# Causal mask of an attention's row maxima: two of four query blocks moved from products on TensorE to a fused add-and-minimum on VectorE

## The chip, the cores and the metric

The kernel runs on one core of a Trainium2 chip. The metric is device microseconds of one execution; less is better. The engines are TensorE (PE; PEld is its weight load), VectorE (DVE), ScalarE (ACT), GpSimd (POOL) and SyncE (SP, which issues most DMAs). A line number, as L626, is that of the kernel's file.

## What is computed

One transformer layer on `x` of (4, 512, 256) with a context of (4, 1601, 256): an attention of 16 heads of 16 columns each, causal, and behind it a layer norm and a feed-forward block with 8 experts (two for each row) and a shared one. The change lies in the attention:

```python
scores = jnp.einsum('bhqd,bhkd->bhqk', Q, K) / jnp.sqrt(jnp.float32(dk))
causal = jnp.tril(jnp.ones((Sq, Sk), dtype=bool))
scores = jnp.where(causal, scores, -jnp.inf)
attn = jax.nn.softmax(scores, axis=-1)
out = jnp.einsum('bhqk,bhkd->bhqd', attn, V)
```

Because of the mask only the first 512 rows of the context count.

## The kernel before

**Groups and slots.** A batch has 512 queries (four blocks k of 128) and 16 heads, handled in four groups of four heads: 16 groups in all, numbered 0 to 15 here in the order in which their maxima are found. For each group the kernel computes the scores twice. First with the queries on the partitions, only to find each row's maximum (kind "R", `rowmax_scores` at L616 on TensorE, `rowmax` at L1296 on VectorE). Then with the keys on the partitions (kind "S", `scoresT` at L638), where the negated maximum of each query is already in the operands as three more rows, so that ScalarE's exponential at L1074 can follow directly, GpSimd clears what lies above the diagonal (L528), and TensorE multiplies with the values (kind "PV", `probs_v`, L654).

**R jobs.** A group has six: two of query block 3 (two heads of 512 keys each), two of block 2 (two heads of 384), one of block 1 (four heads of 256), one of block 0 (four heads of 128); they are called R0 to R5 below, in this order. For each head TensorE makes a product of queries and keys (L624, 96 rows deep, since the float32 operands are split into bf16 parts) and adds to its last 128 columns a product of the identity with a mask tile (L626) that holds 0 up to the diagonal and -1e30 above it. VectorE then reduces the whole job in one instruction to the negated maximum of each row and head (L1306). The jobs alternate between two pairs of accumulator banks (`set_a`): TensorE's job n waits at L617 until VectorE has freed job n - 2.

**From the maxima to the operands.** When all six are reduced, `max_parts` splits the 16 columns of maxima into three bf16 parts (four small instructions, L1312 to L1318). TensorE transposes them (kind "MAX", `maxima`, L634), ScalarE copies the result (L995 called from L1035) and sends it by DMA (L1038) into the operand rows of that group's S jobs.

**The order on TensorE** is written out by hand. In a slot the S jobs of one group, the PV jobs of the group before and the R jobs of the group after are interleaved:

```python
SLOT = [("R", 0), ("PV", 0), ("R", 1), ("PV", 1), ("R", 2),
        ("S", 0), ("R", 3), ("S", 1), ("R", 4), ("S", 2), ("S", 3), ("R", 5), ("S", 4), ("S", 5),
        ("S", 6), ("S", 7), ("PV", 2), ("PV", 3), ("S", 8), ("MAX", 0), ("S", 9), ("S", 10)]
```

The eleven S jobs and the MAX job rotate through three banks (`set_b`); job n waits (L639) until job n - 3 has been read. Every second middle slot is followed by, or follows, the projections of the next batch's queries and keys (L675), and ScalarE splits these into parts within the slot (the copies of L1014 between its exponentials). A batch ends with transposes (L807) and the output projection (L832). The first group's R jobs have no slot around them. After the attention come routing and the experts, which the change doesn't touch.

**Constants.** GpSimd fills the identity, the mask and other constants at the start (L464 to L480); TensorE waits for them (L686) and then repeats a product without use (L684, `keep_busy`) until its first input is there.

Of the kernel before, what the change touches and what calls it, by code (L numbers as in the profile page):

```python
# [28 lines left out]
P = 128  # L29
F32 = mybir.dt.float32  # L30
F32R = mybir.dt.float32r
BF16 = mybir.dt.bfloat16
I32 = mybir.dt.int32
ALU = mybir.AluOpType
ACT = mybir.ActivationFunctionType
AX = mybir.AxisListType
# [3 lines left out]
MASKED = -1e30  # L40
LOWEST = -3e38
# [3 lines left out]
def build(nc, x, ctxT, wqT, bq, wkT, bk, wvT, bv, woT, bo, gwT, wupT, wdnT, sgT, suT, sdT, out):  # L45
    B, S, D = x.shape
    H = NUM_HEADS
    DK = D // H
    HG = P // 32
# [25 lines left out]
    ROWS = DK * len(Q_PART)  # L75
# [4 lines left out]
    with ExitStack() as ctx:  # L80
        def sb(name, shape, dt=F32):
            return ctx.enter_context(nc.sbuf_tensor(name, shape, dt))

        def sem(name):
            return ctx.enter_context(nc.semaphore(name))
# [8 lines left out]
        A = ctx.enter_context(nc.psum_tensor("set_a", [P, 4, 512], F32))  # L94
# [11 lines left out]
        gw = sb("gate_w", [P, C, 32])  # L106
        ident = sb("ident", [P, P])
        identb = sb("identb", [P, P], BF16)
        maskb = sb("maskb", [P, P], BF16)
        beforeb = sb("beforeb", [P, P], BF16)  # L110
        onesb = sb("onesb", [P, P], BF16)
        expert_of = sb("expert_of", [P, NT], I32)
# [40 lines left out]
        def part(words):  # L153
            lo = used[0]
            used[0] += words
            assert used[0] <= size[0], used[0] / KB
            return region[0][:, lo:lo + words]
# [10 lines left out]
        qstack = part(2 * HH * S // 2).bitcast(BF16).rearrange("p (a h n) -> p a h n", a=2, h=HH)  # L168
        kstack = part(2 * HH * S // 2).bitcast(BF16).rearrange("p (a h n) -> p a h n", a=2, h=HH)
# [5 lines left out]
        mneg = part(QT * HG).rearrange("p (k h) -> p k h", k=QT)  # L175
# [15 lines left out]
        bqc = part(2)  # L191
        bkc = part(2)
        zeros = part(D + WHO)

        xs = [attn, attnT.rearrange("p c (k d) -> p (c k) d", d=D)]

# [26 lines left out]
        tot, tiles_of, ends, base = (part(E) for _ in range(4))  # L223
# [24 lines left out]
        consts, pads, fills, pad_rows = sem("consts"), sem("pads"), sem("fills"), sem("pad_rows")  # L248
# [13 lines left out]

        a_full, a_free, b_full, b_free = sem("a_full"), sem("a_free"), sem("b_full"), sem("b_free")
        p_masked, rc_ready, pool_turns = sem("p_masked"), sem("rc_ready"), sem("pool_turns")

        lt_full, lt_read, lg_read, logits_full, route, d_ready, ex_ready, sel_ready = (sem(n) for n in
            ("lt_full", "lt_read", "lg_read", "logits_full", "route", "d_ready", "ex_ready", "sel_ready"))
# [49 lines left out]

        assert A_ALL % 2 == 0
        MAX_AT = 9
        FIRST = [("R", 0), ("R", 1), ("R", 2), ("S", 0), ("R", 3), ("S", 1), ("R", 4), ("S", 2), ("R", 5)]  # L320
        FIRST += [(kind, n) for kind, n in SLOT if kind == "MAX" or kind == "S" and n > 2]
        for order in (SLOT, FIRST):
# [19 lines left out]
        def pair(bank_set, n):  # L342
            return bank_set[:, n % 2 * 2:n % 2 * 2 + 2, :]
# [118 lines left out]
        def _(pool):  # L462
            g = nc.gpsimd
# [2 lines left out]
            g.affine_select(out=ident[:], in_=ident[:], compare_op=ALU.not_equal, fill=1.0, base=0,  # L466
                            pattern=[[-1, P]], channel_multiplier=1).then_inc(consts, 1)
            g.memset(identb[:], 0.0).then_inc(pads, 1)
            g.memset(maskb[:], 0.0).then_inc(pads, 1)
            g.memset(beforeb[:], 0.0).then_inc(pads, 1)  # L470
            g.memset(onesb[:], 1.0).then_inc(pads, 1)
            g.memset(gw[:], 0.0).then_inc(pads, 1)
# [1 line left out]
            g.affine_select(out=identb[:], in_=identb[:], compare_op=ALU.not_equal, fill=1.0, base=0,  # L474
                            pattern=[[-1, P]], channel_multiplier=1).then_inc(consts, 1)

            g.affine_select(out=maskb[:], in_=maskb[:], compare_op=ALU.is_ge, fill=MASKED, base=0,
                            pattern=[[-1, P]], channel_multiplier=1).then_inc(consts, 1)

            g.affine_select(out=beforeb[:], in_=beforeb[:], compare_op=ALU.is_ge, fill=1.0, base=0,  # L480
# [122 lines left out]
        def _(pe):  # L603
            mm, tr = nc.tensor.matmul, nc.tensor.transpose
# [11 lines left out]
            def rowmax_scores(g, j, n, par):  # L616
                pe.wait_ge(a_free, n - 1)  # L617
                k, h0, heads = R_JOBS[j]
                w = (k + 1) * P
                in_bank = heads // 2 if k else HG  # L620
                for i in range(heads):
                    h = g % 2 * HG + h0 + i
                    dst = pair(A, par)[:, i // in_bank, i % in_bank * w:(i % in_bank + 1) * w]
                    mm(dst, qstack[0:ROWS, g // 2, h, k * P:w], kstack[0:ROWS, g // 2, h, 0:w],  # L624
                       start=True, stop=False)
                    last = mm(dst[:, k * P:w], identb[:], maskb[:], start=False, stop=True)  # L626
                last.then_inc(a_full, 1)

            def maxima(n, par, g_count, first=False):
# [236 lines left out]
            last = [logits(b) for b in range(B - 1)][-1]  # L866
# [20 lines left out]
            for t in range(T):  # L887
                last = mm(Bk[:, 3, 0:E], onesb[:], selb[:, t, :], start=t == 0, stop=t == T - 1)
# [325 lines left out]
        def _(dve):  # L1214
            v = nc.vector
# [79 lines left out]

            def rowmax(j, n, par):  # L1296
                k, h, heads = R_JOBS[j]
                dve.wait_ge(a_full, n + 1)
                if k:
                    src = pair(A, par)[:, :, 0:heads // 2 * (k + 1) * P].rearrange("p a (h n) -> p a h n",  # L1300
                                                                                 h=heads // 2)
                    dst = mneg[:, k, h:h + heads].rearrange("p (a h) -> p a h", a=2)
                else:
                    src = pair(A, par)[:, 0, :].rearrange("p (h n) -> p h n", h=HG)
                    dst = mneg[:, k, :]
                v.tensor_reduce(dst, src, AX.X, ALU.max, negate=True).then_inc(a_free, 1)  # L1306

            def max_parts(n, g_count):

# [10 lines left out]
            for g in range(2):  # L1320
                for j in range(A_GRP):
                    n = 3 + g * A_GRP + j
# [135 lines left out]
            for k, oh in enumerate((oh1, oh2)):  # L1458
# [7 lines left out]
                                        op0=ALU.mult, op1=ALU.add))  # L1466
# [178 lines left out]
```

## Time and profile before

| | |
|---|---|
| median of 3 runs | 502.17 us (502.12 to 503.55) |
| the profiled execution | 502.17 us, of it a span of 500.3 us from the first to the last instruction |
| busy share of the span | PE 92%, PEld 64%, DVE 62%, ACT 42%, POOL 39% |
| chain that ended last | PE 68%, DVE 10%, ACT 9%, DMA 6%, issue 5% |
| attention | about 25 to 259 us of the span |

How to read the views: in the groups by line a row is a kind of instruction with its count, busy time and mean duration, and the idle time of its engine just before. In the timeline a row is one instruction, or several of a kind merged, with its start in us of the span, its length, and in brackets the idle time before it and what ended that. The chain of waits is followed back from the end: each piece is what the next one had waited for. The duration of a matmul includes the time until its result has left the array; products behind each other start closer together than that.

### The profile page before, as it was taken

The page shows a single profiled execution, that of the slowest core. Times are in us where ns is not written, and L with a number is a line of the kernel's source. Part 1 is how long each engine was busy: PE and PEld are TensorE (multiplying, and loading weights), DVE is VectorE, ACT ScalarE, POOL GpSimd, SP SyncE. Part 2 cuts the span into 40 slices and gives each one's busy share as a digit, 9 for nine tenths or more (in the row PEclk, how much of TensorE's full clock was granted, in tenths as well). Part 3 has the DMA queues.
Part 4 walks back from the last instruction along what each step waited for, and adds up shares of the span by engine and source line. Part 5 has one row for each costly group of instructions (what it writes and reads, how often), then busy time and mean ns, then how long its engine had stood idle before and what let it go on. Part 6 is the DMA issues. An engine that isn't in the chain of part 4 may idle for free.

```text
span 500.3 us, 10299 instructions
## 1 busy us (share of the span) xinstructions
PE 458.4 (92%) x3154; PEld 318.9 (64%) x3155; DVE 308.2 (62%) x651; ACT 210.1 (42%) x420; POOL 193.1 (39%) x204
## 2 busy tenths in 40 slices
PE   7868999999999999988699799999999999999993
PEld 6644344654447443554256366599999999999852
DVE  4984757477563757656674796855554554555436
ACT  2254666517572566517862352523322322322210
POOL 4123545114541336201512002126666766665420
PEclk9998999999999999999979899999999999999998
DMA  8593322422124121400298900014344344444279
GB/s 263 102 229 107 108 72 65 149 65 73 64 78 145 33 95 47 138 28 2 77 371 292 367 2 21 21 33 65 64 74 74 63 71 70 70 65 74 33 197 338
DMA packets 45574, 53.84 MB, mean 108 GB/s; under 512 B 7760, under 2 KB 41872, under 8 KB 44912
## 3 DMA queue, kind: packets, MB, share of 16 engines
q1 hardware_dynamic: 34320, 39.77, 24.8%
q0 software_dynamic: 7488, 10.31, 12.8%
q10 hardware_dynamic: 3744, 3.47, 2.7%
q8 instruction: 13, 0.21, 0.2%
q14 instruction: 9, 0.07, 0.1%
HBM read 27.09 MB, written 13.67 MB: 81 GB/s over the span
## 4 chain that ended last, share of the span: by engine, by line
PE 68%; DVE 10%; ACT 9%; DMA 6%; issue 5%; SPq 1%; DVEq 0%; ACTq 0%; POOLq 0%
PE set_a L624 7%; PE set_b L654 7%; PE set_a L924 6%; PE set_a L925 5%; PE set_a L923 5%; ACT attention L1074 5%; PE set_a L851 5%; PE set_a L675 4%; PE set_b L644 4%; DVE attention L1306 3%; PE set_b L861 3%; PE set_b L942 3%; PE set_a L832 3%; PE set_b L943 3%; PE set_b L944 3%
## 5 line engine op out<-in xcount | busy, mean ns | idle before, releaser
L1306 DVE TENSOR_REDUCE attention<-set_a 128x2 f32<-128x1024 f32 (+2 forms) x96 | 95.9, 1042 | 28.0 <-PE set_a L626 26.1
L1074 ACT ACTIVATE attention<-set_b 128x512 f32<-128x512 f32 (+1 forms) x176 | 88.4, 570 | 58.5 <-PE set_b L644 45.8
L528 POOL TENSOR_SCALAR_AFFINE_SELECT attention<-attention 128x512 f32<-128x512 f32 x64 | 40.8, 650 | 110.4 <-ACT attention L1074 110.4
L588 POOL DMA_INDIRECT sum_rows<-moe,token_of x39 | 61.8, 1585 | 43.9 <-issue 28.9
L644 PE MATMUL set_b<-attention 99*128 99x512 bf16 (+3 forms) x256 | 60.4, 310 | 13.6 <-ACT attention L1074 10.2
L624 PE MATMUL set_a<-attention 96*128 96x512 bf16 (+3 forms) x256 | 61.5, 306 | 5.6 <-DVE attention L1306 5.4
L580 POOL DMA_INDIRECT e_x<-normed_rows,token_of x39 | 39.4, 1010 | 63.7 <-DVE token_of L1504 37.3
L1173 ACT ACTIVATE moe<-set_a 128x384 f32<-128x384 f32 x39 | 19.1, 490 | 104.9 <-PE set_a L925 104.9
L1529 DVE TENSOR_TENSOR moe<-set_a,moe 128x384 f32<-128x384 f32 x39 | 21.8, 558 | 62.7 <-ACT moe L1173 62.7
L624 PEld LDWEIGHTS set_a<-attention 96*128 96x128 bf16 x256 | 25.3, 99 | 45.3 <-DVE attention L1306 18.0
L923 PE MATMUL set_a<-wup_hi,e_xT_hi 128*128 x156 | 53.1, 340 | 0.0
L924 PE MATMUL set_a<-wup_lo,e_xT_hi 128*128 x156 | 52.9, 339 | 0.0
L925 PE MATMUL set_a<-wup_hi,e_xT_lo 128*128 x156 | 52.8, 338 | 0.0
L626 PE MATMUL set_a<-maskb,identb 128*128 128x128 bf16 x256 | 49.6, 222 | 0.0
L654 PE MATMUL set_b<-attention 128*32 128x128 f32 (+3 forms) x512 | 46.2, 463 | 0.4 <-ACT attention L995 0.3
L644 PEld LDWEIGHTS set_b<-attention 99*128 99x128 bf16 x256 | 19.6, 99 | 37.2 <-ACT attention L1074 24.8
L942 PE MATMUL set_b<-w_down_hi,e_hT_hi 128*128 x117 | 36.4, 311 | 1.3 <-DVE moe L1541 0.8
L995 ACT ACTIVATE attention<-set_b 12x512 bf16<-12x512 f32 (+4 forms) x48 | 25.7, 596 | 22.6 <-PE set_b L820 10.2
L509 POOL TENSOR_TENSOR attention<-attention 128x512 f32<-128x512 f32 x14 | 15.9, 1154 | 47.5 <-ACT attention L995 27.8
L944 PE MATMUL set_b<-w_down_hi,e_hT_lo 128*128 x117 | 32.9, 281 | 0.0
L943 PE MATMUL set_b<-w_down_lo,e_hT_hi 128*128 x117 | 32.9, 281 | 0.0
L995 ACT ACTIVATE attention<-attention 128x512 bf16<-128x512 f32 x32 | 19.4, 644 | 30.9 <-DVE attention L1254 26.2
(167 smaller groups left out, 843.5 us busy)
## 6 DMA issues: line engine op xcount, KB each, us to landing
attention<-attention SPq DMA_DIRECT2D x182, 64.0 KB, 2.6
wup<-in_wupT SPq DMA_DIRECT2D x2, 3072.0 KB, 14.6
sum_rows<-attention SPq DMA_DIRECT2D x2, 2048.0 KB, 13.6
wup<-sum_rows SPq DMA_DIRECT2D x8, 512.0 KB, 7.0
attention<-in_ctxT SPq DMA_DIRECT2D x7, 512.0 KB, 6.2
w_down<-in_wdnT SPq DMA_DIRECT2D x3, 1024.0 KB, 5.0
x_res<-in_x SPq DMA_DIRECT2D x4, 512.0 KB, 7.1
out<-x_res ACTq DMA_DIRECT2D x8, 256.0 KB, 4.0
```

Source lines behind the costliest of these rows:

```text
L588: g.indirect_dma_start(acc[i], bass.IndirectOffsetOnAxis(token_of[:, t:t + 1], 0), e_y[:, t % 2, :], None, compute_op=ALU.add).then_inc(ad ...
L624: mm(dst, qstack[0:ROWS, g // 2, h, k * P:w], kstack[0:ROWS, g // 2, h, 0:w], start=True, stop=False)
L626: last = mm(dst[:, k * P:w], identb[:], maskb[:], start=False, stop=True)
L644: last = mm(bank(par)[:, i * w:(i + 1) * w], kstack[0:ROWS + 3, g // 2, h, k * P:(k + 1) * P], qstack[0:ROWS + 3, g // 2, h, k * P:S], sta ...
L654: last = mm(pv_bank[32 * h:32 * h + 32, k * P:S], vaug[:, k, HG * g + h, :], pT[k][:, h, :], start=k == 0, stop=k == QT - 1, tile_position ...
L923: mm(dst, e_xT_hi[:, a, c, :], wup_hi[:, c, cols], start=c == 0, stop=False)
L924: mm(dst, e_xT_hi[:, a, c, :], wup_lo[:, c, cols], start=False, stop=False)
L925: last = mm(dst, e_xT_lo[:, a, c, :], wup_hi[:, c, cols], start=False, stop=c == C - 1)
L942: mm(dst, e_hT_hi[:, a, m, :], wdn_hi[:, m, cols], start=m == 0, stop=False)
L943: mm(dst, e_hT_hi[:, a, m, :], wdn_lo[:, m, cols], start=False, stop=False)
L1074: nc.scalar.activation(pT[k][:, h:h + heads, :], bank(par)[:, 0:heads * (S - k * P)], ACT.Exp).then_inc(b_free, 1)
L1306: v.tensor_reduce(dst, src, AX.X, ALU.max, negate=True).then_inc(a_free, 1)
```

## The change

For query blocks 0 and 1 (R5 and R4) TensorE makes the score products alone. VectorE then handles each head by itself: an instruction that adds a row of mask values to the head's scores in place (in the accumulator banks), multiplies by -1 and keeps the smallest value of each row, which is the negated maximum. The mask row is 512 wide, zero but for its last 128 columns, which are the old mask tile. A semaphore instruction on VectorE carries the wait for TensorE. Blocks 2 and 3 stay as they were. The mask's place in memory moves from a tensor of its own to the region of the attention.

```diff
-        maskb = sb("maskb", [P, P], BF16)
...
+        mask_row = part(S // 2).bitcast(BF16)
+        maskb = mask_row[:, S - P:S]
...
+        dve_turns = sem("dve_turns")
...
+        MASKED_BY_PE = 2
...
-            g.memset(maskb[:], 0.0).then_inc(pads, 1)
+            g.memset(mask_row, 0.0).then_inc(pads, 1)
...
-                    mm(dst, qstack[0:ROWS, g // 2, h, k * P:w], kstack[0:ROWS, g // 2, h, 0:w],
-                       start=True, stop=False)
-                    last = mm(dst[:, k * P:w], identb[:], maskb[:], start=False, stop=True)
+                    last = mm(dst, qstack[0:ROWS, g // 2, h, k * P:w], kstack[0:ROWS, g // 2, h, 0:w],
+                              start=True, stop=k < MASKED_BY_PE)
+                    if k >= MASKED_BY_PE:
+                        last = mm(dst[:, k * P:w], identb[:], maskb, start=False, stop=True)
...
             def rowmax(j, n, par):
                 k, h, heads = R_JOBS[j]
+                w = (k + 1) * P
+                in_bank = heads // 2 if k else HG
                 dve.wait_ge(a_full, n + 1)
-                if k:
-                    src = pair(A, par)[:, :, 0:heads // 2 * (k + 1) * P].rearrange("p a (h n) -> p a h n",
-                                                                                 h=heads // 2)
+                if k >= MASKED_BY_PE:
+                    src = pair(A, par)[:, :, 0:in_bank * w].rearrange("p a (h n) -> p a h n", h=in_bank)
                     dst = mneg[:, k, h:h + heads].rearrange("p (a h) -> p a h", a=2)
-                else:
-                    src = pair(A, par)[:, 0, :].rearrange("p (h n) -> p h n", h=HG)
-                    dst = mneg[:, k, :]
-                v.tensor_reduce(dst, src, AX.X, ALU.max, negate=True).then_inc(a_free, 1)
+                    v.tensor_reduce(dst, src, AX.X, ALU.max, negate=True).then_inc(a_free, 1)
+                    return
+                dve.sem_inc(dve_turns)
+                for i in range(heads):
+                    src = pair(A, par)[:, i // in_bank, i % in_bank * w:(i % in_bank + 1) * w]
+                    last = v.tensor_tensor_reduce(out=src, in0=src, in1=mask_row[:, S - w:S], scale=-1.0,
+                                                  scalar=-LOWEST, op0=ALU.add, op1=ALU.min,
+                                                  accum_out=mneg[:, k, h + i:h + i + 1])
+                last.then_inc(a_free, 1)
```

## Rows read from the trace of the kernel before

**Rows 1.** The page: busy time by engine, and shares of the chain.
```profile
PE 458.4 (92%) x3154; PEld 318.9 (64%) x3155; DVE 308.2 (62%) x651; ACT 210.1 (42%) x420; POOL 193.1 (39%) x204
...
PE 68%; DVE 10%; ACT 9%; DMA 6%; issue 5%; SPq 1%; DVEq 0%; ACTq 0%; POOLq 0%
```
**Rows 2.** Groups by line and form: busy us, mean ns | idle before, releaser.
```profile
L626 PE MATMUL set_a<-maskb,identb 128*128 128x128 bf16 x256 | 49.6, 222 | 0.0
L1306 DVE TENSOR_REDUCE attention<-set_a 128x2 f32<-128x1024 f32 x32 | 38.3, 1220 | 23.4 <-PE set_a L626 23.4
L1306 DVE TENSOR_REDUCE attention<-set_a 128x2 f32<-128x768 f32 x32 | 29.2, 952 | 2.2 <-PE set_a L626 1.5
...
L1306 DVE TENSOR_REDUCE attention<-set_a 128x4 f32<-128x512 f32 x16 | 10.9, 681 | 0.0
```
**Rows 3.** Chain of waits in a middle slot (start us, us, what).
```profile
121.05 0.97 DVE attention L1306
...
122.34 0.06 PE set_a L626
...
123.17 0.04 ACT attention L1074
```
**Rows 4.** Timeline of VectorE, same slot: R2 and R3, R4, R5, the splitting.
```profile
121.05 1.82 DVE L1306 TENSOR_REDUCE attention<-set_a 128x2 f32<-128x768 f32 x2
...
122.95 1.23 DVE L1306 TENSOR_REDUCE attention<-set_a 128x4 f32<-128x1024 f32 x1
...
124.09 0.68 DVE L1306 TENSOR_REDUCE attention<-set_a 128x4 f32<-128x512 f32 x1
124.81 0.27 DVE L1312 CAST attention<-attention 128x16 bf16<-128x16 f32 x1
...
125.53 0.18 DVE L1318 TENSOR_TENSOR attention<-attention 128x16 bf16<-128x16 f32 x1
```
**Rows 5.** Timeline of TensorE, same slot: the maxima and the last score job.
```profile
126.07 0.39 PE L634 MATMUL set_b<-identb,attention 128*12 128x128 bf16 x4
...
126.83 0.40 PE L644 MATMUL set_b<-attention 99*128 99x128 bf16 x4
```
**Rows 6.** Timeline of VectorE at 20 us: small operations without a wait between them.
```profile
20.20 0.17 DVE L1223 TENSOR_TENSOR mean<-stats 128x12 f32<-128x12 f32 x1
20.28 0.18 DVE L1224 TENSOR_TENSOR st_c<-stats 128x12 f32<-128x12 f32 x1
```
**Rows 7.** Groups by line and form, GpSimd: the fill of the mask tile.
```profile
L469 POOL MEMSET maskb<- 128x128 bf16 x1 | 0.2, 197 | 0.0
```
**Rows 8.** Chain of waits at the start of the program.
```profile
4.89 8.55 DMA x_res<-in_x
```
**Rows 9.** Timeline of TensorE at the end of a batch.
```profile
92.68 0.40 PE L644 MATMUL set_b<-attention 99*128 99x128 bf16 x4
93.24 0.32 PE L807 MATMUL set_a<-ident,attention 128*128 128x128 f32 x1 [0.17 <-ACT attention L995]
```
**Rows 10.** Timeline of VectorE and TensorE, a slot in which ScalarE splits operands.
```profile
115.26 0.18 DVE L1318 TENSOR_TENSOR attention<-attention 128x16 bf16<-128x16 f32 x1
...
117.07 0.40 PE L644 MATMUL set_b<-attention 99*128 99x128 bf16 x4 [0.57 <-ACT attention L1074]
```
**Rows 11.** Timeline of TensorE, group 0: its maxima.
```profile
34.08 0.39 PE L634 MATMUL set_b<-identb,attention 128*12 128x128 bf16 x4 [0.71 <-DVE attention L1318]
```
**Rows 12.** Timeline of TensorE and VectorE, group 1.
```profile
40.24 0.32 PE L626 MATMUL set_a<-maskb,identb 128*128 128x128 bf16 x1
...
44.35 0.17 DVE L1318 TENSOR_TENSOR attention<-attention 128x16 bf16<-128x16 f32 x1
...
44.58 0.39 PE L634 MATMUL set_b<-identb,attention 128*12 128x128 bf16 x4
```
**Rows 13.** Timeline of VectorE and TensorE, group 14.
```profile
228.79 0.18 DVE L1318 TENSOR_TENSOR attention<-attention 128x16 bf16<-128x16 f32 x1
...
231.46 0.34 PE L644 MATMUL set_b<-attention 99*128 99x128 bf16 x3 [0.48 <-ACT attention L1074]
```

More of the change, by code:

```diff
@@ L475, in _ @@
                             pattern=[[-1, P]], channel_multiplier=1).then_inc(consts, 1)
-            g.affine_select(out=maskb[:], in_=maskb[:], compare_op=ALU.is_ge, fill=MASKED, base=0,
+            g.affine_select(out=maskb, in_=maskb, compare_op=ALU.is_ge, fill=MASKED, base=0,
                             pattern=[[-1, P]], channel_multiplier=1).then_inc(consts, 1)
```

## The prediction

> **What bounds the kernel now.** I read the page's engine totals and chain first: TensorE is busy for 92% of the span and holds 68% of the chain, VectorE 62% and 10% [rows 1]. That makes every product removed look like a gain, and VectorE look free; neither holds before the stage itself is read. The groups by line and form come next [rows 2]: 256 products with the mask (line 626), of which the change takes 128 away, and the reductions of line 1306. The 0.22 us shown for one mask product is latency. In the chain such a product takes only 0.06 us between two score products [rows 3], so the 128 are worth at most 128 x 0.06 = 7.7 us of TensorE's queue, if all of them lay on the path.
>
> They do not. Call the six row-maximum jobs of a group R0 to R5; R4 is query block 1 (four heads of 256 keys), R5 block 0 (four heads of 128). The chain through a middle slot goes from VectorE's reduction of R2 to R4's products, to the first transposed-score product behind them and to ScalarE's exponentials [rows 3]. R4's four mask products are on it, 4 x 0.06 = 0.24 us. R5's are not: behind them TensorE waits for the exponentials, which follow each other on ScalarE. So the gain is 0.24 us for a slot, and the other 0.24 us vanishes in a wait.
>
> VectorE's side is where the change puts work. In that slot R4's reduction starts at 122.95 and R5's at 124.09, the splitting of the maxima runs from 124.81 to 125.71 [rows 4], and TensorE takes the maxima (line 634) at 126.07 [rows 5]. That is 0.36 us of room; TensorE's queue is in order, so whatever makes the maxima later than that holds up all that stands behind them.
>
> **The change part by part.** *Mask products:* 8 fewer for a group (and 8 weight loads beside them), 0.24 us on the path as above. R4's data are also ready before VectorE has finished R3: two reductions of 768 take 1.82 us where one takes 0.95 [rows 2, 4], so they follow each other at 0.87 us, and from 121.05 VectorE is ready at 122.79 instead of the 122.95 at which R4 began. R4 begins 0.17 us earlier.
>
> *Fused instructions:* two reductions (1024 and 512 wide) become eight adds with minimum, four 256 wide and four 128 wide. Their price is in no row of this trace, so I bound it. Durations of 1220 and 952 ns for 1024 and 768 columns give 1.047 ns a column [rows 2]; with 0.87 us from start to start for 768, each instruction adds 0.066 us. By that 256 columns cost 0.334 and 128 cost 0.200, the eight 2.14 us. The end of the last is seen later than its pace says: R5 takes 0.72 us until the next instruction starts [rows 4], against 512 x 1.047 + 66 = 0.60, so 0.12 more. Then 2.26 us stand against today's 124.81 - 122.95 = 1.86. *Lower bound: D = 0.40 us* more on VectorE for a group, in case the second output (one minimum for each row) is free.
>
> An instruction that writes a full tile and also one value for each partition has two outputs of different shape. The nearest rows for writing so little are 12-column operations that follow each other without a wait, 0.08 us from start to start [rows 6]. Charging 0.08 for each of the eight gives 0.64 more: *D = 1.04 us, the value I take*, since the minimum has to be written somewhere and these are the rows nearest to it. *Upper bound:* the in-place write into the accumulator banks keeps the instructions from overlapping, so that each pays what a lone one pays, 681 - 536 = 0.145 us instead of 0.066 [rows 2]: 8 x 0.08 = 0.64 more, D = 1.68.
>
> The Trainium skill (VectorE: DVE Perf Modes, section Two Vector instructions with no wait between them) says that an operation which also writes out its accumulator is two instructions, the main one and a read of the accumulator; no run here shows it, and by it the sum would be the one at D = 1.04.
>
> *The semaphore step* on VectorE ahead of each fused job is an instruction of the sequencer that waits for TensorE and can run while the instruction before it computes; both jobs' data are there early, so I cost it at nothing. Without that cover it costs a few hundredths of a microsecond and belongs to the upper part of the range. *The longer fill* of the mask row on GpSimd (512 columns instead of 128; the small one takes 0.2 us [rows 7]) delays TensorE's first products by some tenths, but the chain at that time waits for the input rows until 13.45 [rows 8]: nothing. No DMA is added; the maxima's rows leave ScalarE's queue behind a copy that is itself behind the next exponential, so their transfer moves with the slot.
>
> *What is late next, slot by slot.* A step of D reaches the path only where the maxima come behind what holds TensorE today.
> - Three middle slots followed by a projection (groups 3, 7, 11): after the maxima come a score job (0.32 + 0.24 us until the last one can start) and the last score job, at 126.83 today [rows 5], which waits for an exponential. With the maxima ready at 125.71 - 0.17 + D + 0.05 it starts at 126.15 + D: a shift of D - 0.68, or -0.24 if that is less.
> - Three that end a batch (5, 9, 13): behind the last score job (0.23 us, from 92.68) the transposes wait for ScalarE until 93.24 [rows 9], which is 0.33 us more room: D - 1.01.
> - Six slots in which ScalarE also splits the operands (2, 4 to 12 even): the last score job waits 0.57 us for ScalarE [rows 10]; from 115.44, the end of the splitting, the same steps give 115.88 + D against 117.07: D - 1.19.
> - The first two groups have no room. In the first, TensorE waits 0.71 us for the maxima [rows 11]: D - 0.24. In the second TensorE runs at half its clock up to R4 (a mask product shows 0.32 us instead of 0.22), so R4 comes 0.43 sooner; there is 0.06 us of room before the maxima [rows 12], and behind them I put 0.13: D - 0.62.
> - The last two groups are bound by ScalarE, on which the last score job waits 0.48 us there [rows 13]; the steps above give 229.41 + D against its start at 231.46, so no D below 1.8 reaches it: -0.24 each.
>
> At D = 1.04: 3 x 0.36 + 3 x 0.03 - 6 x 0.15 + 0.80 + 0.42 - 0.48 = **+1.0 us**. The profiled execution took 502.17 us (a span of 500.3 and 1.9 around it), which is also the median of the runs, so **503.2 us**: no change that can be told. A measurement of this kernel tells 0.3%, or 1.5 us, from no change.
>
> **The rivals.**
> *The second output is free* (D = 0.40): every middle slot keeps its 0.24 us. 12 x -0.24 + 0.16 - 0.22 - 0.48 = -3.4: 498.8 us, faster. For it: one instruction, and reductions write their result at no visible cost. Against it: a reduction has only that one output.
> *The fused instructions don't overlap, and the maxima become the wait* (D = 1.68): 3 x 1.00 + 3 x 0.67 + 6 x 0.49 + 1.44 + 1.06 - 0.48 = +10.0: 512 us, slower. It decides from D = 1.08, where the sum passes 1.5 us; above D = 1.2 each 0.1 us costs 1.4 us, since 14 of 16 groups pay. For it: this kernel has no VectorE write into these banks, so nothing excludes it. Against it: reads from there overlap today.
> The Trainium skill (Perfetto Trace Analysis, section Optimizing Scalar/DVE Operations) gives about 125 ns of overhead for a VectorE instruction on PSUM, which would put D near 1.5 and the time near 509.5, an estimate from that page; the trace's own 0.066 us for reductions that read PSUM speaks against it.
> *Reading and writing one bank halves the rate* (D = 1.04 + 4 x 384 x 1.047 ns = 2.65): +25 us, 527. Nothing in the trace shows an engine doing both in one bank.
>
> **How the numbers follow.** The forecast, D between 0.7 and 1.2, gets 0.42: 500.1 to 505.4, with 0.06 of it below -1.5 us and 0.09 above +1.5. The free second output gets 0.27, the lost overlap 0.25, the halved rate 0.06. Faster: 0.27 + 0.06 = 0.33; within: 0.27; slower: 0.09 + 0.25 + 0.06 = 0.40. The range reaches from 498.5 to 512 and leaves out half of the lost overlap's upper end, the halved rate and what lies below the free output.
>
> **What would show it.** Right: 128 products of line 626 instead of 256; eight fused instructions for a group with some 0.41 us (256) and 0.28 us (128) from start to start, or a small separate row behind each; the splitting of the maxima about 0.9 us later behind R4's start; TensorE waiting for line 1318 ahead of line 634 in the odd middle groups and hardly in the even ones; the first score job behind R4 0.24 us sooner after R2's reduction. Wrong: starts 0.33 and 0.20 apart with no row behind them (then faster), 0.5 and 0.4 or more apart (then slower), or a wait ahead of line 634 in all fourteen groups.

## The result, and the profile after

The changed kernel takes 534.68 us (median of 4 runs, 532.6 to 538.09) against 502.75 us for the kernel before on the same chip (4 runs, 502.12 to 503.55): a ratio of 1.0656, 95% interval 1.0617 to 1.0696, 31.9 us slower. (The ratio, to which the interval belongs, isn't the quotient of the two medians, which is 1.0635.) The prediction, 503.2 us in a range of 498.5 to 512, was wrong by far. The profiled execution below took 532.76 us, a span of 530.8.

The page of the kernel after, its busy times by engine and the shares of its chain:

```profile
PE 467.7 (88%) x3026; PEld 318.1 (60%) x3027; DVE 336.0 (63%) x875; ACT 212.3 (40%) x420; POOL 195.1 (37%) x204
...
PE 62%; DVE 23%; DMA 5%; ACT 5%; issue 3%; SPq 1%; DVEq 0%; POOLq 0%
```

TensorE has 128 matmuls fewer than in [rows 1] and is busy 9 us *longer*; VectorE's share of the chain has more than doubled, from 10 to 23%. The groups by line and form of the kernel after say what VectorE does with it (busy us, mean ns | idle before):

```profile
L1313 DVE CUSTOM_DVE_ANT_0 set_a<-set_a,attention 128x256 f32<-128x256 f32 x64 | 25.3, 457 | 1.8 <-PE set_a L627 1.8
...
L1313 DVE DVE_READ_ACCUMULATOR2_ANT attention<- 128x1 f32 x128 | 18.1, 141 | 0.0
...
L1313 DVE CUSTOM_DVE_ANT_0 set_a<-set_a,attention 128x128 f32<-128x128 f32 x64 | 17.2, 332 | 0.0
...
L1326 DVE CAST attention<-attention 128x16 bf16<-128x16 f32 x16 | 8.7, 546 | 0.6
...
L1324 DVE TENSOR_TENSOR attention<-attention 128x16 f32<-128x16 f32 x16 | 8.3, 516 | 0.5
...
L1328 DVE TENSOR_TENSOR attention<-attention 128x16 bf16<-128x16 f32 x16 | 8.2, 513 | 0.5
```

The fused instructions of line 1313 are there, each with a small row behind it that reads the accumulator out. But the surprise is in the last three rows: the operations that split the maxima, which the change doesn't touch and which took 0.18 us before [rows 4], now take over 0.5 us in the mean. The waits of TensorE say where that lands (us in total, times, longest):

```profile
PE set_b L638 <- DVE attention L1328: 26.4, 14, 2.8
```

Line 638 is the transposition of the maxima (634 before), line 1328 the last step of the splitting: TensorE waits for it in all fourteen groups 0 to 13, where before it waited 0.71 us in group 0 [rows 11], 0.12 us in group 1 and not at all behind that.

The timeline shows what holds the splitting up. First the slot that [rows 3 to 5] show (group 7) in the kernel after, VectorE, GpSimd and TensorE (start us, us):

```profile
135.98 0.43 DVE L1313 CUSTOM_DVE_ANT_0 set_a<-set_a,attention 128x256 f32<-128x256 f32 x1
...
137.29 0.64 POOL L531 TENSOR_SCALAR_AFFINE_SELECT attention<-attention 128x512 f32<-128x512 f32 x1 [5.06 <-ACT attention L1078]
...
137.48 0.33 DVE L1313 CUSTOM_DVE_ANT_0 set_a<-set_a,attention 128x128 f32<-128x128 f32 x1
...
138.22 0.33 DVE L1313 CUSTOM_DVE_ANT_0 set_a<-set_a,attention 128x128 f32<-128x128 f32 x1
...
138.65 0.17 DVE L1322 CAST attention<-attention 128x16 bf16<-128x16 f32 x1
138.83 0.64 POOL L531 TENSOR_SCALAR_AFFINE_SELECT attention<-attention 128x512 f32<-128x512 f32 x1 [0.90 <-ACT attention L1078]
138.86 0.63 DVE L1324 TENSOR_TENSOR attention<-attention 128x16 f32<-128x16 f32 x1
...
139.52 0.17 DVE L1326 CAST attention<-attention 128x16 bf16<-128x16 f32 x1
...
140.04 0.38 PE L638 MATMUL set_b<-identb,attention 128*12 128x128 bf16 x4 [1.02 <-DVE attention L1328]
```

R4 starts at 135.98 and the splitting at 138.65: 2.67 us, where it was 1.86 [rows 4]. Then the second small operation begins 0.03 us behind a select of GpSimd's and takes 0.63 us instead of 0.18; it ends when the select does, at 139.47 to 139.49. Now group 8 of the same kernel, an even group, in whose slot GpSimd also computes third pieces of the LayerNorm (line 517):

```profile
152.56 0.17 DVE L1322 CAST attention<-attention 128x16 bf16<-128x16 f32 x1
152.74 0.63 POOL L531 TENSOR_SCALAR_AFFINE_SELECT attention<-attention 128x512 f32<-128x512 f32 x1 [0.89 <-ACT attention L1078]
152.76 0.63 DVE L1324 TENSOR_TENSOR attention<-attention 128x16 f32<-128x16 f32 x1
...
153.34 2.26 POOL L517 TENSOR_TENSOR attention<-attention 128x512 bf16<-128x512 f32 x2
153.43 1.09 DVE L1326 CAST attention<-attention 128x16 bf16<-128x16 f32 x1
...
154.56 1.08 DVE L1328 TENSOR_TENSOR attention<-attention 128x16 bf16<-128x16 f32 x1
...
155.77 0.59 PE L638 MATMUL set_b<-identb,attention 128*12 128x128 bf16 x4 [2.84 <-DVE attention L1328]
```

Three operations of 16 columns in a row, each lasting until the GpSimd operation beside it ends, and a wait of 2.84 us on TensorE. All six even middle groups (2 to 12) look like this, with 2.83 or 2.84 us; all six odd ones (3 to 13) like group 7, with 1.02 us. In groups 14 and 15 no GpSimd operation lies beside the splitting, and TensorE doesn't wait for it.

In the kernel before, the splitting of group 7 ran from 124.81 to 125.71 [rows 4]. GpSimd's rows of that stretch, from its timeline:

```profile
124.42 0.64 POOL L528 TENSOR_SCALAR_AFFINE_SELECT attention<-attention 128x512 f32<-128x512 f32 x1 [3.65 <-ACT attention L1074]
125.95 0.64 POOL L528 TENSOR_SCALAR_AFFINE_SELECT attention<-attention 128x512 f32<-128x512 f32 x1 [0.90 <-ACT attention L1074]
```

The splitting lay almost wholly in the 0.9 us between two selects. Its first operation began while the earlier one still ran, and took 0.27 us instead of 0.17.

A second thing differs. The granted clock of TensorE by stretches of 50 us (windows of the two traces; 1 is 2.4 GHz, and the level below is half, 1.2 GHz):

| us of the span | 0–50 | 50–100 | 100–150 | 150–200 | 200–250 | 250–300 | at half, us |
|---|---|---|---|---|---|---|---|
| before | 0.97 | 1.00 | 1.00 | 1.00 | 1.00 | 0.90 | 13 |
| after | 0.93 | 0.93 | 0.97 | 0.86 | 0.90 | 0.90 | 51 |

The last column is worked out: 100 us times what is missing to 1, summed over the six.

### The profile page after: what moved, and what is told of

Read it like the earlier page. It is cut to its first block, busy times and chain, and to the rows that moved or that the text cites. A ratio compares the mean times of both kernels' runs of the same rounds, so it can differ in the third digit from the quotient of the medians.

```text
span 530.8 us, 10299 instructions
## 1 busy us (share of the span) xinstructions
PE 467.7 (88%) x3026; PEld 318.1 (60%) x3027; DVE 336.0 (63%) x875; ACT 212.3 (40%) x420; POOL 195.1 (37%) x204
## 4 chain that ended last, share of the span: by engine, by line
PE 62%; DVE 23%; DMA 5%; ACT 5%; issue 3%; SPq 1%; DVEq 0%; POOLq 0%
PE set_a L627 6%; PE set_b L658 6%; PE set_a L928 5%; PE set_a L929 5%; PE set_a L927 5%; DVE attention L1308 4%; PE set_a L679 4%; DVE set_a L1313 4%; PE set_b L648 4%; PE set_a L855 3%; PE set_b L946 3%; PE set_a L836 3%; PE set_b L947 2%; PE set_b L948 2%; PE set_b L865 2%
## 5 line engine op out<-in xcount | busy, mean ns | idle before, releaser
L531 POOL TENSOR_SCALAR_AFFINE_SELECT attention<-attention 128x512 f32<-128x512 f32 x64 | 42.5, 677 | 134.8 <-ACT attention L1078 134.8
L1308 DVE TENSOR_REDUCE attention<-set_a 128x2 f32<-128x1024 f32 (+1 forms) x64 | 66.7, 1085 | 29.5 <-PE set_a L630 28.8
L648 PE MATMUL set_b<-attention 99*128 99x512 bf16 (+3 forms) x256 | 63.2, 326 | 10.0 <-ACT attention L1078 6.6
L627 PE MATMUL set_a<-attention 96*128 96x512 bf16 (+3 forms) x256 | 59.4, 321 | 5.7 <-DVE attention L1308 5.5
L627 PEld LDWEIGHTS set_a<-attention 96*128 96x128 bf16 x256 | 22.5, 102 | 54.0 <-DVE attention L1308 31.8
L658 PE MATMUL set_b<-attention 128*32 128x128 f32 (+3 forms) x512 | 51.3, 505 | 0.4 <-ACT attention L999 0.3
L999 ACT ACTIVATE attention<-set_b 12x512 bf16<-12x512 f32 (+4 forms) x48 | 27.6, 601 | 42.1 <-PE set_b L638 15.5
L648 PEld LDWEIGHTS set_b<-attention 99*128 99x128 bf16 x256 | 22.8, 105 | 34.0 <-ACT attention L1078 22.6
L1313 DVE CUSTOM_DVE_ANT_0 set_a<-set_a,attention 128x256 f32<-128x256 f32 (+1 forms) x128 | 41.2, 394 | 1.8 <-PE set_a L627 1.8
```

Of the source, the lines that this page charges most:

```text
L627: last = mm(dst, qstack[0:ROWS, g // 2, h, k * P:w], kstack[0:ROWS, g // 2, h, 0:w], start=True, stop=k < MASKED_BY_PE)
L648: last = mm(bank(par)[:, i * w:(i + 1) * w], kstack[0:ROWS + 3, g // 2, h, k * P:(k + 1) * P], qstack[0:ROWS + 3, g // 2, h, k * P:S], sta ...
L658: last = mm(pv_bank[32 * h:32 * h + 32, k * P:S], vaug[:, k, HG * g + h, :], pT[k][:, h, :], start=k == 0, stop=k == QT - 1, tile_position ...
L999: copy = lambda o, i: nc.scalar.activation(o, i, ACT.Copy)
L1313: last = v.tensor_tensor_reduce(out=src, in0=src, in1=mask_row[:, S - w:S], scale=-1.0, scalar=-LOWEST, op0=ALU.add, op1=ALU.min, accum_ou ...
```

## The experiments

**Theory:** the fused instructions cost about what was forecast. They make the splitting 0.8 us later, into GpSimd's next operations, each of which holds up one operation of the splitting to its end; TensorE idles behind it and then loses half its clock for a while. **Rivals:** the fused instructions themselves (their length, the write into the bank they read); the lateness alone, without GpSimd; TensorE's own side.

**1. GpSimd's operations behind the splitting.** To the changed kernel:

```diff
...
 for k in range(QT):
+    if k == 1 and found is not None:
+        pool_turn(mparts_ready, found)
     if k == 2 and split is not None:
         part3(split)
...
```

`pool_turn` is a wait of GpSimd on a semaphore, here the one that the splitting raises when it is over; the calls hand over in `found` which group's splitting it is.

> The changed kernel, with one wait more on GpSimd: from the second select of a group's probabilities on, and so also the third pieces of the LayerNorm, it runs only when the splitting of the maxima that falls in that slot is over. The DVE work stays: R4's and R5's fused instructions still make the splitting start 2.67 us after R4 instead of 1.86 us. Theory (the splitting is late and meets GpSimd's select and third pieces, which hold it up): the four small operations go back from 3.0 us (even groups) and 1.2 us (odd groups) to 0.7 to 0.9 us, TensorE's wait ahead of MAX falls from 2.83 us in even groups and 1.02 us in odd ones to under 0.7 us, the stretches at half the granted clock shrink from about 51 us of the first 300 us to under 25 us, and the time is 502 to 513 us (about a third of the 32 us may stay as what GpSimd's later selects cost the products with V). Rival 1 (the fused instructions themselves cost the time, by their length or by writing into the bank that they read): waits and time stay, 528 to 536 us. Rival 2 (GpSimd is itself short of time, and moving it only moves the wait): the splitting is short again but the waits turn up ahead of the products with V, 525 to 540 us.

Measured: 502.04 us against 502.20 us of before, ratio 1.0002 (0.9988 to 1.0015). The fused work is all there, and the whole loss is gone. The same slot, group 8, in this kernel's timeline:

```profile
139.03 0.18 DVE L1326 CAST attention<-attention 128x16 bf16<-128x16 f32 x1
139.25 0.17 DVE L1328 TENSOR_TENSOR attention<-attention 128x16 f32<-128x16 f32 x1
139.45 0.18 DVE L1330 CAST attention<-attention 128x16 bf16<-128x16 f32 x1
139.66 0.17 DVE L1332 TENSOR_TENSOR attention<-attention 128x16 bf16<-128x16 f32 x1
...
139.97 0.38 PE L642 MATMUL set_b<-identb,attention 128*12 128x128 bf16 x4 [0.56 <-DVE attention L1332]
140.16 0.64 POOL L533 TENSOR_SCALAR_AFFINE_SELECT attention<-attention 128x512 f32<-128x512 f32 x1 [1.84 <-ACT attention L1003]
```

The four operations are back to 0.17 or 0.18 us, R4 to the splitting is still 2.66 us, and the wait is 0.56 us in every middle group. The time at half clock, worked out as in the table above, is back at 13 us. Rivals 1 and 2 of this run fall.

**2. Late without fused instructions.** To the kernel before, two plain reductions more for a group:

```diff
+if k == 1:
+    v.tensor_reduce(spare[:, 0:2], ...[:, 0, 0:512]..., AX.X, ALU.max, negate=True)
+if k == 0:
+    v.tensor_reduce(spare[:, 2:3], ...[:, 0, 0:128]..., AX.X, ALU.max, negate=True)
 v.tensor_reduce(dst, src, AX.X, ALU.max, negate=True).then_inc(a_free, 1)
```

> The kernel before, all masks as products on PE and all maxima as plain reductions, with two more plain reductions per group whose result is not used: 512 columns of R4's scores and 128 of R5's. By the lengths of the reductions there (1024 columns in 1.14 us, 512 in 0.72 us, start to start) that is some 0.8 us more of VectorE between R4 and the splitting, as much as the fused instructions add (0.81 us). Theory (it is the lateness of the splitting alone, whatever makes it late, that brings it under GpSimd's operations): the splitting takes up to 3 us in even groups here too, TensorE waits 2 to 3 us ahead of MAX there, and the time is 522 to 538 us. Rival 1 (the fused instruction, its accumulator read or its write into the bank): the splitting stays near 0.9 us and the time is 502 to 508 us, the 0.8 us less the 0.36 us of room and the slack of the odd groups. Rival 2 (the missing mask products on PE, by a PE that is idle and loses its clock): 502 to 508 us as well, with the half clock's stretches as before, 13.7 us.

Measured: 519.59 us, ratio 1.0340 (1.0319 to 1.0362): a little under the theory's range, far above the rivals'. Group 8 in its timeline:

```profile
146.30 0.64 POOL L529 TENSOR_SCALAR_AFFINE_SELECT attention<-attention 128x512 f32<-128x512 f32 x1 [3.00 <-ACT attention L1075]
...
146.57 0.28 DVE L1311 TENSOR_REDUCE attention<-set_a 128x1 f32<-128x128 f32 x1
146.77 0.68 DVE L1313 TENSOR_REDUCE attention<-set_a 128x4 f32<-128x512 f32 x1
...
147.48 0.17 DVE L1319 CAST attention<-attention 128x16 bf16<-128x16 f32 x1
...
147.69 0.17 DVE L1321 TENSOR_TENSOR attention<-attention 128x16 f32<-128x16 f32 x1
147.83 0.63 POOL L529 TENSOR_SCALAR_AFFINE_SELECT attention<-attention 128x512 f32<-128x512 f32 x1 [0.89 <-ACT attention L1075]
147.90 0.59 DVE L1323 CAST attention<-attention 128x16 bf16<-128x16 f32 x1
...
148.43 2.27 POOL L515 TENSOR_TENSOR attention<-attention 128x512 bf16<-128x512 f32 x2
148.53 1.09 DVE L1325 TENSOR_TENSOR attention<-attention 128x16 bf16<-128x16 f32 x1
...
149.75 0.38 PE L635 MATMUL set_b<-identb,attention 128*12 128x128 bf16 x4 [1.72 <-DVE attention L1325]
```

The same hold-ups without a single fused instruction. R4 to the splitting is 2.65 us (144.83 to 147.48), as late as in the kernel after. The splitting starts 0.35 us ahead of the second select here (147.48 to 147.83) and 0.18 us in the kernel after, so two of its operations are caught in even groups, not three, and TensorE waits 1.72 instead of 2.83 us. The reductions, which read the accumulator banks, run beside the first select at their usual length (the 512-wide one 0.68 us, as in [rows 4]): not every VectorE instruction is held.

**3. TensorE's side alone.** From the kernel before, the mask products of blocks 0 and 1 left out (`if k >= 2:` ahead of line 626), nothing in their place.

> The kernel before with the mask products of the two lower query blocks left out and nothing in their place: the maxima of these blocks are taken over unmasked scores, so the mask of the maxima of blocks 0 and 1 is the part left out. VectorE's plain reductions stay as they are. This is the change's side on PE alone. The prediction's step: R4's four mask products are on the path with 0.24 us a slot and R5's are hidden, 15 slots, so 3 to 4 us, 498 to 500 us. Rival 1 (all eight products are on the path, 0.48 us a slot): 494 to 496 us. Rival 2 (TensorE is not what bounds there, the products only filled time in which VectorE was late): 501.5 to 503 us.

Measured: 499.12 us against 502.20, ratio 0.9947 (0.9930 to 0.9964): 3.1 us, near the 0.24 us a slot and far from the 7.7 us of all products. The traces show it by the slot: from R4 of group 2 to R4 of group 13, eleven slots, it is 146.62 us instead of 149.25, 0.24 us for each.

**4. The clock.** The changed kernel, with products that nobody reads ahead of the maxima:

```diff
...
+    for _ in range(filler):
+        mm(bank(par)[:, 0:P], identb[:], beforeb[:], start=True, stop=True)
     pe.wait_ge(mparts_ready, g_count)
...
```

> The changed kernel, with products that nobody reads put on TensorE ahead of MAX in the slots where it waits there: 44 of 128 columns where an even group's splitting is waited for, 16 where an odd group's is, into the bank that MAX is about to overwrite. The wait for the splitting is as long as before, but TensorE works through it. Theory (of the 32 us one part is the waits themselves, about 2.8 us in six even groups and 1 us in six odd ones, some 23 us, and the rest the half clock that follows them): the stretches at half the granted clock shrink from about 51 us of the first 300 us to under 20 us, and the time falls by 8 to 18 us, to 515 to 526 us. Rival 1 (the half clock costs nothing because VectorE or GpSimd set the pace in those slots): clock restored, time 531 to 536 us. Rival 2 (the granted clock doesn't follow the waits): stretches at half clock stay, and the time is 533 to 540 us.

Measured: 519.48 us, ratio 1.0341 (1.0314 to 1.0367), 15.2 us less than the changed kernel. The windows of 150 to 200 us, first of the kernel after, then of this one (busy us of PE, PEld, DVE, ACT and POOL with their instructions, then the granted clock, DMA share, GB/s):

```profile
150.00:200.00 50.00, 42.00 (x265) 22.54 (x264) 31.30 (x81) 22.70 (x46) 13.68 (x18) 0.86 0.22 74
```

```profile
150.00:200.00 50.00, 47.70 (x398) 28.28 (x395) 34.03 (x85) 24.13 (x49) 13.05 (x17) 1.00 0.26 86
```

The splitting is as long as in the kernel after (3.08 us in even groups, 1.26 in odd ones), yet from 50 to 200 us the clock stays at 1.00. Over the six stretches of the table above this kernel has 0.93, 1.00, 1.00, 1.00, 0.93, 0.93: 21 us at half instead of 51. So TensorE's idling behind the splitting is what brought the clock down. The Trainium skill (TensorE: Matmul & The Clock Gate, Part 1) says that the clock is set by how busy TensorE has lately been. The traces agree: from 150 to 200 us 0.86 with the waits and 1.00 with products in them.

**5 and 6. Block 1 alone.** The changed kernel with R5 back on mask products and a plain reduction (`stop=k == 1`, `if k != 1:` around the mask product and the reduction), once as it is and once with the wait of experiment 1.

> The changed kernel with the fused add-and-maximum for block 1 (R4) alone; block 0 (R5) goes back to mask products on PE and one plain reduction. R5's four products were hidden anyway, so PE's gain of 0.24 us a slot stays, and the splitting comes 0.39 us later than in the kernel before (four times 0.382 us less 1.14 us), not 0.81. Theory (what costs is that the splitting meets GpSimd): in the kernel before, the splitting of an even group ran from 56.83 to 57.73 us, between a select that ended at 57.07 and the next that began at 57.97; moved by 0.39 us, less what the selects move, its last operation begins right at the second select. If it slips ahead of it the time is 498 to 501 us, as the step at 0.39 us gives; if it falls behind, the select and a third piece are added, 0.6 to 1.7 us in each even group, and the time is 504 to 515 us. Rival (the fused instruction as such costs the time, by its form or by writing into the bank it reads): half of what it cost with both blocks, 515 to 520 us.

> Block 1 alone by the fused instruction, as in the run beside it, and GpSimd's second to fourth selects and third pieces behind the group's splitting, as in the run of the changed kernel with that wait (502.04 us, TensorE waiting 0.56 us ahead of MAX in every group). Theory: the splitting takes 0.7 us and comes 0.41 us earlier than there, so the wait ahead of MAX falls to 0.15 us or less and the gain of R4's products (3 us when they are left out alone) comes through: 498 to 500 us, faster than the kernel before by 0.4 to 0.9%. Rival (the wait put on GpSimd costs as much as it gives, as 502.04 for 500.8 by the sum suggested): 501 to 503 us.

Measured: 498.89 us, ratio 0.9942 (0.9922 to 0.9963), and 498.63 us, ratio 0.9948 (0.9924 to 0.9972), against 501.95 us. Both are about 3 us faster than the kernel before, which is what leaving the lower blocks' products out gave in experiment 3. The first is on the edge, though. From its timeline, the last operation of the splitting in groups 9 and 11:

```profile
147.24 0.68 POOL L531 TENSOR_SCALAR_AFFINE_SELECT attention<-attention 128x512 f32<-128x512 f32 x1 [0.90 <-ACT attention L1078]
147.24 0.17 DVE L1332 TENSOR_TENSOR attention<-attention 128x16 bf16<-128x16 f32 x1
...
147.54 0.38 PE L638 MATMUL set_b<-identb,attention 128*12 128x128 bf16 x4
...
180.91 0.63 POOL L531 TENSOR_SCALAR_AFFINE_SELECT attention<-attention 128x512 f32<-128x512 f32 x1 [0.90 <-ACT attention L1078]
180.91 0.65 DVE L1332 TENSOR_TENSOR attention<-attention 128x16 bf16<-128x16 f32 x1
...
181.70 0.38 PE L638 MATMUL set_b<-identb,attention 128*12 128x128 bf16 x4 [0.60 <-DVE attention L1332]
```

Both start in the same hundredth of a microsecond as a select. In group 9 VectorE goes first, 0.17 us; in group 11 GpSimd does, and the same operation takes 0.65. In the second kernel no middle group has this.

**7. The wait alone,** as a control: experiment 1's edit in the kernel before.

> The kernel before, all masks on PE, with GpSimd's wait for the splitting alone, as a control: whether that wait gives or costs time of itself. Theory: in the kernel before, TensorE waited 0.00 us ahead of MAX in groups 2 to 15, so shorter splitting gives nothing, and the selects lie behind the splitting there already: 501.5 to 503 us, no change. Rival 1 (the splitting was held up in the kernel before too, its first operation 0.28 instead of 0.17 us, and that was on the path): 499 to 501 us. Rival 2 (the wait delays the products with V): 503.5 to 507 us.

Measured: 501.59 us, ratio 1.0007 (0.9985 to 1.0028): no change. The wait gives nothing by itself; it only takes the hold-up away where there is one.

**8. Third pieces alone** put behind the splitting (the wait of experiment 1 at `k == 2`, for the even groups).

> The changed kernel, with only GpSimd's third pieces of the LayerNorm (two operations of 1.15 us, in the slots that hold an even group's maxima) put behind the splitting; the selects stay where they are. This tells the share of the third pieces from that of the selects. Theory: in even groups one operation of the splitting still sits behind a select (0.63 us) and the other two go back to 0.17 us, so TensorE's wait ahead of MAX is about 1.0 us there, as in odd groups; 12 groups with 0.45 us more than with both moved (502.04 us) is 5.5 us, and up to 8 us of half clock with it: 506 to 516 us. Rival (the selects are what costs, the third pieces only lengthen what is waited for anyway): 525 to 534 us.

Measured: 509.12 us, ratio 1.0159 (1.0123 to 1.0194). Even groups now wait 1.02 us as the odd ones do; the total of that row of waits falls from 26.4 to 14.9 us:

```profile
PE set_b L640 <- DVE attention L1330: 14.9, 14, 1.4
```

So some 25 of the 32 us hang on the third pieces, with the half clock that follows them, and the rest on the selects.

**9 and 10. A dose of 0.2 us.** Block 1 alone with one plain reduction of 128 columns more ahead of R5's, without and with GpSimd's wait.

> Block 1 alone by the fused instruction (498.89 us, splitting ahead of GpSimd's next select by 0.2 us in all middle groups but one), and on VectorE one plain reduction of 128 columns more ahead of R5's, whose result is not used: 128 x 1.047 ns + 0.066 us = 0.20 us later for the splitting, and no other difference. Theory (a cliff: where the last small operations fall behind a running GpSimd operation each waits for its end): in the middle groups at least the last of the four starts behind the select and takes 0.6 us, TensorE's wait ahead of MAX goes from 0.11 to some 0.8 us, and the time is 505 to 512 us; if the last two fall behind, the last in even groups waits for a third piece too, and it is 512 to 520 us. Rival (lateness itself, in proportion): 0.20 us in 14 groups at most, 499 to 502 us.

> The same 0.20 us more on VectorE, in the kernel with block 1 alone by the fused instruction and GpSimd's wait for the splitting (498.63 us). Theory: no cliff, because the selects and third pieces stand behind the splitting whenever it comes: the splitting takes 0.7 us, TensorE's wait ahead of MAX goes from 0.11 to about 0.3 us, and the time is 498.6 to 501.5 us. Rival (what the run beside it loses is not GpSimd): the same loss as there, over 504 us.

Measured: 500.35 us, ratio 0.9976 (0.9958 to 0.9995), and 499.23 us, ratio 0.9957 (0.9931 to 0.9983), against 501.62 us. For the first the theory's number missed: the time fell into the rival's range, so the time alone doesn't exclude that rival, and the intervals of the two runs overlap. What tells them apart is the trace, of the longest of the ten executions (504.42 us). Group 9:

```profile
150.33 0.65 POOL L532 TENSOR_SCALAR_AFFINE_SELECT attention<-attention 128x512 f32<-128x512 f32 x1 [0.90 <-ACT attention L1079]
150.52 0.49 DVE L1335 TENSOR_TENSOR attention<-attention 128x16 bf16<-128x16 f32 x1
...
151.14 0.38 PE L639 MATMUL set_b<-identb,attention 128*12 128x128 bf16 x4 [0.62 <-DVE attention L1335]
```

The hold-up is there in the middle groups, and the last operation takes 0.47 to 0.49 us in all but one of them. But only the rest of a select that already ran for 0.19 us counts, 0.3 us, where I had charged the whole select; and most slots have room that takes such a delay up. The splitting takes 1.11 us instead of 0.90 and starts 2.41 us behind R4 instead of 1.86, so it ends 0.55 + 0.21 = 0.76 us later than in the kernel before. By the slot terms of the prediction that is 3 x 0.08 for groups 3, 7 and 11, -0.24 for the nine other middle groups and -0.14 for groups 0, 1, 14 and 15 together: -2.1 us. Measured: -1.2 (0.24% of 501.62). So the loss begins gently; it becomes large when several operations are caught and no room is left. For the second run the theory held: TensorE waits some 0.3 us in all middle groups but one, and no operation of the splitting takes more than 0.18 us.

## Why the prediction was wrong, step by step

**What held.** *The gain:* 0.24 us a slot from R4's products, none from R5's; leaving both out measured 3.1 us (experiment 3), and R4's alone, with the fused instruction in their place, about as much (5 and 6). *The fused instructions:* 256 wide ones start 0.382 us apart and 128 wide ones 0.249 us, with a read of the accumulator behind each that overlaps the next, against 0.41 and 0.28 forecast. D, the time from R4 to the splitting, rose by 2.67 - 1.86 = 0.81 us, between the lower bound of 0.40 and the 1.04 taken. The Trainium skill's sentence that an instruction with an accumulator output is two (VectorE: DVE Perf Modes, section Two Vector instructions with no wait between them) is borne out by the 128 rows of 0.14 us. Its 125 ns of overhead for a VectorE instruction on the accumulator banks (Perfetto Trace Analysis, section Optimizing Scalar/DVE Operations) put D near 1.5, by an estimate, and the runs show 0.81: an instruction and its read together cost 0.114 us over their columns (0.382 less 256 x 1.047 ns). *The write into the bank that is read* costs nothing by the column: 0.382 - 0.249 = 0.133 us for 128 columns is the reductions' 1.047 ns a column. By the prediction's own slot terms D = 0.81 gives 3 x 0.13 - 3 x 0.20 - 6 x 0.24 + 0.57 + 0.19 - 0.48, which is -1.4 us: slightly faster.

**The step that failed** is that "the splitting of the maxima runs from 124.81 to 125.71", taken over as a fixed 0.90 us wherever it starts. Every shift of the prediction adds D to the end of the splitting and lets its length stand. What that length rests on was not asked: in the kernel before, it was a gap of 0.90 us between two selects, which ends 0.24 us behind the splitting (125.95 against 125.71). The row that told it was there to be read: the first of the four, with nothing to wait for, at 0.27 us beside a select, where the last took 0.18 [rows 4]. With D = 0.81 the gap is missed; the splitting takes 1.26 us in odd groups and 3.07 us in even ones. A second term is missing: the sum leaves TensorE's clock as it was, and the waits of 1.0 to 2.8 us that follow brought 38 us more at half of it.

The Trainium skill has the rule that speaks against this change (SBUF — State Buffer, section Who interferes with whom): VectorE and GpSimd share one pair of ports, and whichever starts first holds it for its whole instruction. A VectorE instruction with two inputs in SBUF meets a GpSimd instruction that reads SBUF there, and copies and casts can, while a reduction doesn't, nor does an instruction with at most one input in SBUF outside the modes that use both ports. The traces agree: subtractions and casts of 16 columns take 0.5 to 1.1 us beside GpSimd, reductions and the fused instructions beside a select keep their length (0.68 and 0.33 us), and whichever starts first goes first. I had not weighed it, since I saw no GpSimd instruction in the change.

**The ledger.** The prediction's slot terms with the measured lengths: D and what the splitting grew by are 0.81 + 2.17 = 2.98 us in even groups and 0.81 + 0.36 = 1.17 us in odd ones, so 6 x (2.98 - 1.19) + 3 x (1.17 - 0.68) + 3 x (1.17 - 1.01) + 0.57 + 0.32 - 0.48 = 13.1 us. The half clock: 51 - 13 = 38 us more of it, at most 19 us of TensorE's work lost. Together at most 32.1 us; measured 31.9. Experiment 4 with the same splitting and 8 us more at half clock than before: 13.1 + 4 = 17.1; measured 17.3. The traces give the same split without these terms. From R4 of group 2 to R4 of group 13 the kernel before takes 149.25 us at a granted clock of 1.00, experiment 4 takes 162.41 us at 1.00, and the kernel after 176.55 us at 0.91: of the 27.3 us, 13.2 stay with the clock restored and 14.1 go with the clock. So about half of the loss are the waits and the rest is the clock that they cost. Neither the forecast nor any rival named either; the halved rate came nearest with 527 us, by a mechanism that the runs refute.

**The marks.** "TensorE waiting ... in the odd middle groups and hardly in the even ones" came out wrong: both wait, the even ones longer (2.83 us against 1.02); and the mark put down for a wrong prediction, "a wait ahead of line 634 in all fourteen groups", is what the trace shows.

**What stays open.** Experiment 1 came out 0.2 us under the kernel before, where the same slot terms (its splitting takes 0.80 us) give -2.1 us; of the missing 1.9 us the traces put some 0.5 in the middle groups, where groups 3, 7 and 11 had less room than I had put down, 0.4 before group 2 and 1.0 after group 13, and the last two I can't tell from scatter. That the ports are what GpSimd and VectorE share is the Trainium skill's explanation; the runs show who waits for whom, not through what.

## What to carry over

When an operation moves, look at what runs beside it on the other engines at the new place, not only at who waits for it: a duration read from one profile holds for that neighbourhood. Small VectorE operations between buffers belong where GpSimd is idle, or GpSimd's belong behind a semaphore of theirs; here that wait costs nothing and turns 6.6% slower into no change. Move only the part that is on the path: fusing the mask of one block instead of two gave all of the gain with less than half of the lateness (0.36 us instead of 0.81).

## What the hardware showed that I had not expected

A 16-column operation of 0.17 us took 0.5 to 1.1 us beside a running GpSimd operation, and which of two that start in the same hundredth of a microsecond goes first differed between groups of one execution. Stalls of 1.0 to 2.8 us, one a slot, took TensorE to half its clock for 38 us more in all, and that cost about as much as the stalls themselves: filling them with products that nobody reads gave 15.2 us back. An add-and-minimum in place in the accumulator banks takes no longer by the column (1.04 ns) than a reduction that only reads them (1.047 ns).
